# A graph network's second attention layer makes its edges' logits inside its pass; three smaller moves with it

## What is computed

```python
x = layernorm(x + relu(concat([x, segment_sum(w * x[dst], src)]) @ W + b))
x = layernorm(x + gat(gat(x)) @ Wf + bf)           # two attention layers, 4 heads and 1 head
x = layernorm(x + segment_sum(w * (x @ W + b)[src], dst))
x = layernorm(x + gcn3(x))                         # three GCN convolutions

def gat_layer(x, ...):                             # self-loops included
    h = (x @ W).reshape(n, H, C)
    al_s, al_d = (h * a_src).sum(-1), (h * a_dst).sum(-1)
    logits = leaky_relu(al_s[src] + al_d[dst], 0.2)
    out = segment_sum(h[src] * softmax_by_dst(logits), dst) + b
```

## Time and profile before

| | us |
|---|---|
| median of three runs | 8406.1 (8400.13 to 8410.41) |
| the profiled execution | 8404.63, its span 8400.0 |
| PE / PEld busy | 6116.0 (73%) / 4372.8 (52%) |
| POOL busy | 5793.1 (69%) |
| DVE / ACT busy | 3526.4 (42%) / 1570.8 (19%) |
| mean granted TensorE clock | 0.806 |
| L1081, the attention passes' gathers | 1568 of 948 ns |
| L1162, the attention passes' products | 4704 records of rows, 3136 of weights |
| L1846, the logits' scatters | 100 of 974 ns |

### The profile page before, as it was taken

One profiled execution on the slowest core, in us unless ns is written; L12 is line 12 of the kernel. 1 busy time (PEld: TensorE's weight loads), 2 busy tenths in 40 slices (PEclk: granted clock), 3 DMA queues, 4 the chain that ended last, 5 costly groups with the idle time before them and its releaser, 6 DMA issues. The chain is left out here.

```text
span 8400.0 us, 130868 instructions
## 1 busy us (share of the span) xinstructions
PE 6116.0 (73%) x30280; PEld 4372.8 (52%) x30280; DVE 3526.4 (42%) x13701; ACT 1570.8 (19%) x5156; POOL 5793.1 (69%) x5612
## 2 busy tenths in 40 slices
PE   2777777673788883888866666677777777777777
PEld 1444444462466651333335556566666666666665
DVE  3444444352666662555543333322222222223333
ACT  1333333221122220222212222100000000000000
POOL 3888888502677765777757777577776777767776
PEclk9888888786899995777768998778777877867776
DMA  7777777442444431111123444344443444434443
GB/s 244 114 115 115 116 114 114 73 130 70 108 115 114 115 100 20 34 34 34 35 56 117 118 117 118 94 118 117 117 117 107 118 118 117 117 105 118 117 118 107
DMA packets 503634, 871.04 MB, mean 104 GB/s; under 512 B 119784, under 2 KB 348330, under 8 KB 501098
## 3 DMA queue, kind: packets, MB, share of 16 engines
q0 software_dynamic: 331872, 673.49, 35.1%
q1 hardware_dynamic: 171658, 196.42, 7.5%
HBM read 677.39 MB, written 192.10 MB: 104 GB/s over the span
## 5 line engine op out<-in xcount | busy, mean ns | idle before, releaser
L704 PE MATMUL bank<-onehots,rows 128*128 128x128 f32 x12544 | 2526.2, 349 | 925.4 <-DMA rows<-gcn_rows,index 571.3
L648 POOL DMA_INDIRECT rows<-gcn_rows,index x2352 | 2237.5, 951 | 816.3 <-issue 657.4
L704 PEld LDWEIGHTS bank<-onehots,rows 128*128 128x128 f32 x12544 | 2076.1, 242 | 1368.2 <-DMA rows<-gcn_rows,index 732.3
L1081 POOL DMA_INDIRECT rows<-gat_rows,index x1568 | 1487.2, 948 | 587.3 <-issue 434.3
L1330 POOL DMA_INDIRECT support<-rows,index x784 | 1216.5, 1552 | 310.6 <-DMA support<-rows,index 138.6
L1162 PE MATMUL bank<-onehots,rows 128*128 128x128 f32 (+1 forms) x4704 | 995.1, 325 | 294.8 <-DVE rows L1216 293.7
L1162 PEld LDWEIGHTS bank<-onehots,rows 128*128 128x128 f32 (+1 forms) x4704 | 608.1, 186 | 700.4 <-issue 523.0
L648 POOL DMA_INDIRECT rows<-norm,index x784 | 744.3, 949 | 298.7 <-issue 224.6
L735 DVE TENSOR_SCALAR onehots<-iota,half_offset,edge_values 128x128 f32<-128x128 f32 x3136 | 855.5, 361 | 169.0 <-issue 90.5
L745 DVE TENSOR_TENSOR acc<-acc,bank 128x256 f32 x396 | 165.2, 417 | 1360.1 <-PE bank L704 1360.1
L1403 PE MATMUL cross_bank<-same_source,onehots 128*128 128x128 f32 x1568 | 374.3, 326 | 442.7 <-DVE same_source L1460 442.7
(11 more groups left out here) (263 smaller groups left out, 5877.7 us busy)
## 6 DMA issues: line engine op xcount, KB each, us to landing
source_row<-in_src_flat SPq DMA_DIRECT2D x99, 512.0 KB, 5.0
rows<-gcn_rows,index POOLq DMA_INDIRECT x2352, 2.8
support<-zeros POOLq DMA_DIRECT2D x16, 1632.0 KB, 30.2
support_rows<-support SPq DMA_DIRECT2D x40, 640.0 KB, 7.1
rows<-gat_rows,index POOLq DMA_INDIRECT x1568, 2.5
gcn_rows<-out SPq DMA_DIRECT2D x150, 128.0 KB, 1.8
own_rows<-gcn_rows SPq DMA_DIRECT2D x150, 128.0 KB
x_window<-in_x SPq DMA_DIRECT2D x98, 128.0 KB, 2.7
```

What stands on the lines that cost most here:

```text
L648: nc.gpsimd.indirect_dma_start(rows[:, k, :], None, table, bass.IndirectOffsetOnAxis(ap=index[:, k:k + 1], axis=0),).then_inc(gathered[k], 16)
L704: done = nc.tensor.matmul(by_chunk(banks[h])[:, c, :], rows[:, k, c * P:(c + 1) * P], onehots[:, k, :], start=first and c == 0, stop=final ...
L1081: nc.gpsimd.indirect_dma_start(rows[:, k, :], None, table, bass.IndirectOffsetOnAxis(ap=index[:, k:k + 1], axis=0),).then_inc(gathered[k], 16)
```

## The change

- **Logits in the pass.** The second attention layer no longer runs `to_edges` and `lay_out_weights` before its pass. `rows2` gets one column more (the stored rows hold `al_s` and `al_d`), and SP loads, for each half, the window's 128 values of `al_d` and the half's 1024 destinations onto all partitions (512 KB). DVE compares these with the window's lanes (`turned_onehots`: one instruction of 128 x 1024, int32 in, fp32 out), and PE multiplies each tile's turned one-hots by the window's values (`shares`: 8 products with 128 weight columns and 1 moving column). `from_window` has one buffer. The first layer still lays out its logits beforehand, in one more phase.
- **Weights' sums folded.** With one head, the weight goes into the column behind the features, so a tile is one product of 65 columns instead of two, `acc` has 65 partitions, `z` isn't used, the spreading multiplies by ones, and the reciprocal is taken of 64 x 128 values after it (`dve_divide`).
- **The division a turn on.** In both passes, division, bias and `pe_third` of a block move into the next turn, `dve_second` of the normalisation stands further back, and the stores are ordered anew. The blocks left after the loop take one step more, and their steps are interleaved.
- **Zeros.** `zero_scratch` is gone. POOL zeroes `support` in the set-up, after the loads; `scratch` is zeroed and x loaded on SP's queue at the start of the scatter phase, ahead of its loop. POOL then zeroes the small `spare`.
- **Ends of runs.** `degrees` turns only the histogram (50 products), and gets running counts from two products with all blocks' counts, a scan over 50 blocks, and a subtraction.

```diff
 def attention_pass(nc, g, table, kind, inside, **fields):
             @block.sync
+                def load_half(i, n):
+                    h = n % 2
+                    base = sync.value_load(g.half_base[0:1, bass.ds(i * 2 + (n + 1), 1)], ...)
+                    if not (isinstance(i, int) and 2 * i + n < 2):
+                        sync.wait_ge(s.from_window_ready, i * 2 + (n - 1))
+                        sync.wait_ge(s.shared, i * 2 + (n - 1))
+                    sync.dma_start(dst_row[:, h, :], g.dst_flat[...].to_broadcast([P, HALF * P])).then_inc(row_loaded[h], 16)
+                    sync.dma_start(window_share[:, h, :], table[bass.ds(base, P), features + heads:features + 2 * heads],
+                                   ...).then_inc(share_loaded[h], 16)
...
             @block.scalar
+                    kept = (rows[:, batch * BATCH:(batch + 1) * BATCH, features:features + 1] if folded
+                            else edge_weight[:, batch, :, :])
+                    nc.scalar.activation(kept, exponent[:, batch, :, :], ACT.Exp).then_inc(s.weight_kept, 1)
...
             @block.tensor
+                def shares(i, n):
+                    h = n % 2
+                    pe.wait_ge(s.from_window_ready, i * 2 + (n + 1))
+                    pe.wait_ge(share_loaded[h], i * 16 + 16 * (n // 2 + 1))
+                    if not (isinstance(i, int) and 2 * i + n < 2):
+                        pe.wait_ge(s.exponent_ready, i * batches + (n - 1) * per_half)
+                    for k in range(HALF):
+                        done = nc.tensor.matmul(share_banks[h][:, k, :], from_window[:, k, :],
+                                                window_share[:, h, :], start=True, stop=True)
+                    done.then_inc(s.shared, 1)
                 def multiply(i, k):
                     if first:
+                        shares(i, h + 1)
                         pe.wait_ge(s.added, i * 2 + (h + 1))
...
+                        if late is not None and k == 4:
+                            ends.pe_third(pe, s, late)
                         if b is not None and k == 7:
                             ends.pe_first(pe, s, b, i * 2 + 2)
-                        if b is not None and k == 12:
+                        if b is not None and k == 13:
                             ends.pe_second(pe, s, b)
-                    if b is not None:
-                        ends.pe_third(pe, s, b)
...
             @block.vector
+                def turned_onehots(i, n):
+                    dve.wait_ge(row_loaded[n % 2], i * 16 + 16 * (n // 2 + 1))
+                    if not (isinstance(i, int) and 2 * i + n < 1):
+                        dve.wait_ge(s.shared, i * 2 + n)
+                    nc.vector.tensor_scalar(from_window[:].rearrange("p k e -> p (k e)"), dst_row[:, n % 2, :],
+                                            g.window_lane[:, bass.ds(i * 2 + n, 1)], None, ALU.is_equal
+                                            ).then_inc(s.from_window_ready, 1)
                 def turn(i, b=None, late=None):
                     batch_of(i, 0)
+                    turned_onehots(i, 2)
                     add(1, base[0], i * batches + batches, i * 2 + 1)
                     if late is not None:
+                        ends.dve_divide(dve, s, late)
+                    batch_of(i, 1)
+                    if late is not None:
                         ends.dve_late(dve, s, late)
-                    batch_of(i, 1)
                     batch_of(i, 2)
+                    turned_onehots(i, 3)
+                    if late is not None:
+                        ends.dve_later(dve, s, late)
                     if b is not None:
                         ends.dve_invert(dve, s, b)
                         dve.wait_ge(s.cleared, b + 2)
                     add(0, base[1], i * batches + (batches + HALF // BATCH), i * 2 + 2)
                     batch_of(i, 3)
-                    if b is not None:
-                        ends.dve_divide(dve, s, b)
...
 def set_up(nc, g, t, support, zeros):
-                sync.dma_start(g.x[:], t.x...).then_inc(s.x_loaded, 16)
-                sync.wait_ge(s.x_loaded, 16)
+                pool.wait_ge(s.zeros_ready, 1)
+                pool.wait_ge(s.loaded, 16 * 12)
+                        pool.dma_start(target, zeros).then_inc(g.support_zeroed, 16)      # 16 of them
...
 def degrees(nc, g, histogram):
-                nc.vector.tensor_tensor_scan(running[:], one[:].to_broadcast([3, g.blocks * P]), histogram[:], ...)
+                nc.tensor.matmul(totals, ones[:], number[:], start=True, stop=True)
+                nc.tensor.matmul(after, g.earlier[:], number[:], start=True, stop=True).then_inc(s.counted, 1)
```

More of the change, by code:

```diff
@@ L889, in dve_prepare @@
         dve.wait_ge(s.selected, 1)
-        for c in range(self.chunks):
+        if self.folded:
+            done = vector.memset(self.selector[self.width:self.lanes, :, :], 1.0)
+        for c in range(0 if self.folded else self.chunks):
             own_heads = self.g.identity[0:self.heads, c * per_chunk:(c + 1) * per_chunk]
@@ L1037, in dve_late, with dve_later, attention_pass @@
         dve.sem_inc(s.issued, 1)
-        self.normalised.dve(dve, s, b)
-def attention_pass(nc, g, table, kind, **fields):
-    loops, batches = g.tiles // RING, RING // BATCH
+        self.normalised.dve_first(dve, s, b)
+    def dve_later(self, dve, s, b):
+        self.normalised.dve_second(dve, s, b)
+def attention_pass(nc, g, table, kind, inside, **fields):
+    loops, batches, per_half = g.tiles // RING, RING // BATCH, HALF // BATCH
     with ExitStack() as stack:
@@ L1056, in attention_pass @@
         zeros = sbuf("zeros", [P, 2, P])
+        if inside:
+            dst_row = sbuf("dst_row", [P, 2, HALF * P], INT32)
+            window_share = sbuf("window_share", [P, 2, heads])
+            from_window = sbuf("from_window", [P, HALF, P])
+            share_banks = [psum(f"share_bank{h}")[:, 0:HALF * heads].rearrange("p (k h) -> p k h", h=heads)
+                           for h in range(2)]
         banks = [psum(f"bank{h}") for h in range(2)]
@@ L1340, in _ @@
             def _(sync):
+                kept = 0
+                if first_pass:
+                    sync.dma_start(g.x[:], g.x_dram.rearrange("(b p) f -> p b f", p=P)).then_inc(s.kept, 16)
+                    kept += 16
+                    for n, dram in scratch.items():
+                        target = dram.rearrange("(p i) v -> p (i v)", p=P)
+                        for at in range(0, g.tiles * n, zeros.shape[1]):
+                            to = min(at + zeros.shape[1], g.tiles * n)
+                            sync.dma_start(target[:, at:to], zeros[:, 0:to - at]).then_inc(s.kept, 16)
+                            kept += 16
                 with sync.Fori(0, g.tiles // RING) as i:
@@ L1417, in _ @@
             def _(dve):
-                nc.vector.memset(zeros[:], 0.0).then_inc(s.zeroed, 1)
                 if first_pass:
@@ L1539, in groups_after, with set_up @@
     return g.tiles // RING - WITHIN
-def set_up(nc, g, t):
+def set_up(nc, g, t, support, zeros):
     with ExitStack() as stack:
@@ L1566, in set_up @@
         hid = t.L3_gnn_mw2.shape[0]
-        with phase(nc, "loaded", "x_loaded", "iota", "own", "relu", "added", "gated", "kept",
-                   "turned", "wide", "stored") as (block, s):
+        with phase(nc, "loaded", "iota", "own", "relu", "added", "gated", "kept",
+                   "turned", "wide", "stored", "zeros_ready") as (block, s):
             @block.sync
@@ L1898, in _, with attend, lay_out_shares @@
                 link(nc.vector.tensor_copy(g.narrow_range[:], flags[:, 2:3]))
-def attend(nc, g, table, logits, features, heads, segment, scratch, planes, kind, again, before, **fields):
+def attend(nc, g, table, logits, features, heads, segment, scratch, planes, kind, inside, again, before, **fields):
+    def lay_out_shares():
+        with ExitStack() as stack:
+            sbuf, _ = tiles_of(stack, nc)
+            a_dst = sbuf("a_dst", [P, g.blocks, heads])
+            spread = sbuf("spread", [P, g.tiles, heads])
+            filled = sbuf("filled", [P, g.tiles, heads])
+            with phase(nc) as (block, s):
+                @block.vector
+                def _(dve):
+                    nc.vector.tensor_copy(a_dst[:], g.self_logits[:, :, heads:2 * heads])
+            to_edges(nc, g, a_dst, heads, scratch[heads], spread, filled)
+            lay_out_weights(nc, g, filled, None, spread, heads, planes)
     attention_bound(nc, g, heads)
@@ L1941, in _, with beforehand @@
                     nc.scalar.activation(own, own, ACT.Exp)
-            to_edges(nc, g, a_dst, heads, scratch[heads], spread, filled)
-            lay_out_weights(nc, g, filled, None, spread, heads, planes)
-        attention_pass(nc, g, table, kind, features=features, heads=heads, **fields)
+        if not inside:
+            lay_out_shares()
```

(5 more changed lines are left out.)

308 lines of the change are left out of this document (184 added, 124 removed).

## The result

The changed kernel takes 8327.1 us (8319.9 to 8333.3) against 8406.6 for the kernel before on the same chip: 0.9906, interval 0.9895 to 0.9918. The forecast was 8432. The change made the kernel 0.94% faster, and the sign of the forecast was wrong. The profiled execution spans 8315.2 us, 84.8 under the 8400.0 of before.

A forecast was written before the change was run, and what follows sets the result against it. It took gathers to bound the second pass before, and a DVE-PE chain at the low clock after. Terms of -146 outside that loop and +172 in it, on 8404.6 plus 1.5, gave 8432 us, range 8320 to 8500.

The forecast's parts named there:

- The loop: Second attention pass: turns go from 20.4 to 24.1 us, adding 172 us (120 to 240).
- PE together 15.9: Second pass: PE's shares, odd batches and block work take 15.9 us a turn at the low clock, 8.0 at the high.
- a product after another shape takes 0.73: Second pass on PE: price in us of a product following one of another shape, at the low clock.
- four restarts after another shape 0.8: Second pass, PE's odd batches: 0.8 us a turn for four restarts, on top of 3.4 for 8 tiles.
- the 2.4 for the two products: Second pass, the block's two products with 256 moving columns: 0.62 us each at the high clock, 2.4 at the low one.
- the forecast's 24.1: Second pass: expected us a turn, mostly at the low clock, with about 1 us of PE's work at the high one.
- Rival C: Second pass: high clock on 3 us of PE's work, 22.0 us a turn, +75, 8335 us in all; chance 0.17.
- The chain through the single buffer: Second pass: each half turn runs shares, DVE's stretch, odd batch and block, shares; 25.2 us a turn at the low clock.
- rival E: Second pass: the shares' passes take half of 0.213 us also at the low clock, 20.7 a turn, 8274 us; chance 0.02.
- The sign named for POOL: Second pass's gathers: "issue" gives way to PE as their releaser, 1.5 us each instead of 1.28.
- under the gate's work on DVE and ACT, which holds the set-up to about 42 as before: Set-up: POOL's zeros run beside this work, the set-up still ends near 42 us; part of the zeros' -20 us.
- 39 MB at 424 GB/s from 18.5: Set-up and scatter's start: zeros, x and scratch load from 18.5 to 110 us; part of the zeros' -20 us.

The follow-up runs named there:

- narrow_products_b: The changed kernel with second-pass products 64 weight columns wide instead of 65 and 64 accumulator rows transposed, neighbours' weight sum left out: 8411.9 us, 1.0016 of the kernel before.
- two_buffers_b: The changed kernel with a second buffer for the turned one-hots, on a chip without pauses: 8262.6 us, 0.9833 of the kernel before.
- wide_moving_b: The changed kernel with 128 moving columns instead of 1 in each product of the shares, on a chip without pauses: 8252.7 us, 0.9821 of the kernel before.
- logits_before_b: The changed kernel with the second layer's logits laid out ahead of its pass again, no shares inside it, without pauses: 8326.6 us, 0.9909 of the kernel before.
- support_zeros_back: The changed kernel with POOL's 16 zero writes of support requested at the head of the scatter again instead of in the set-up: 8339.8 us, one run.

## Why the prediction was wrong, point by point

**The loop, the step that failed.** "PE together 15.9" was too long, above all in "a product after another shape takes 0.73", which I put on the transposition (2 x 0.73), on "four restarts after another shape 0.8" and in the 2.4 for the two products. The 0.73 was read from a kernel whose accumulator had 64 rows, and the change makes them 65. I noted the new shape and took the old shape's price. Measured are 13.9 (6.6 + 7.35): the transposition 0.8 instead of 1.5, the two products 2.16 instead of 2.4, the odd batches 3.8 instead of 4.2, the shares 0.65 less.

narrow_products_b has the shapes of the forecast's prices and tells how much of this is the width. In the whole pass it is 84 (1152.2 against 1068.0) of the 104 us by which the loop was overestimated (172 against 68.1), 1.7 us a turn. In a turn all at the low clock it is 1.3: forecast 25.2, narrow_products_b 24.0, changed kernel 22.7. The other 1.2 of such a turn are terms taken too long even for the old shapes: DVE's stretches (9.3, measured 8.9), the shares (7.2, measured 7.0), the products and batches (8.8, measured 8.1). The rest of the 1.7 is the clock, high for a while in every second turn of the changed kernel and almost never in the narrow one. So that the forecast's 24.1 stands close to narrow_products_b's 23.5 is partly luck: it had taken off 1.1 for a high clock that this kernel didn't have, which made up for the terms taken too long.

That turned the sign, since slower turned into faster at 23.5 us a turn: the forecast stood 0.6 above its own point of change, and the width is worth 1.7. Rival C (22.0 a turn, 8335) had the number, but by luck: it wanted the high clock on 3 us of PE's work; the clock was 0.54. Two slips in the sum changed little: 47 x (24.1 - 20.4) is 174, not 172, and four restarts at 0.73 instead of 0.43 are 1.2, not 0.8.

**What held in the loop.** The chain through the single buffer (two_buffers_b), the turned one-hots at 0.75 (forecast 0.8), the shares' pass at 0.213 against rival E, the low clock (under 0.6). Of its cause half held: products with 128 moving columns in the shares raise it (wide_moving_b), but without shares it is as low (0.53, logits_before_b). The sign named for POOL didn't come: "issue" did not give way to PE. It is still the largest part, PE has 3.3 us, the late gathers come through the index copy (61.2 us), and the gathers follow at 1.36 us (1068.0 over 783), not 1.5. The forecast also took 20.05 as the floor, which no kernel with the one long building reached: it holds up the gathers beside it.

**Zeros: -11.7 instead of -20.** The step that failed is "under the gate's work on DVE and ACT, which holds the set-up to about 42 as before". POOL's DRAIN holds the phase until what POOL has requested has landed (support_zeros_back: x requested at 36.6 without, 83.4 with), so x and `scratch` start only then. "39 MB at 424 GB/s from 18.5" was wrong with it: the zeros were requested at 14.9, and the window from 70 to 124 has 361 GB/s.

**Degrees -36, logits ahead of the pass -96, ends of passes:** right within 6 us. What I took as their sum, -146, was -152.9; 5.2 of that lies in passes that the change doesn't touch, and nothing here explains it.

## What to carry to other kernels

When a change alters the shape of an operation by even one row or column, a price read from its old neighbours no longer holds: look at what the shapes on both sides of each start will be. When the sum stands near the point at which the sign turns, the range of its largest term decides, not its middle. And when two engines hand a single buffer to and fro, price the chain that this makes, and look for every way to shorten it: here a second buffer (0.9833), a faster clock (0.9821) and products without gaps (0.9819) each brought the turn to the same 20.5.

## What the runs showed of the hardware that I had not expected

- Where the weight rows or columns go from 64 to 65 or 128 or back, the products start some 0.3 us late at the low clock (0.73 instead of 0.43 from L851 to L852); with 65 instead of 64 on one side and 128 on the other, they don't.
- A DVE `tensor_scalar` over 1024 columns holds up a gather that POOL starts during it by up to 0.5 us; with eight of 128 columns no gather takes over 1.1 us.
- A phase doesn't end before POOL's requested DMAs have landed: POOL's DRAIN lasted 61.1 us, to 0.7 us after the last landing, and ACT stood idle for 47 us, DVE for 50.
- The shares' 16 products with one moving column each leave the clock low; the same products with 128 moving columns take it from 0.54 to 0.77, and the time from 0.9906 to 0.9821 of the kernel before. Without shares it was 0.53.
- Chips differ: the kernel before has medians of 8398 to 8407 us on most of them and of 9706 to 9784 on three, by pauses between instructions from the first attention pass on.
